# Attention values with 32-column stationary tiles, softmax sums from a block of ones, masked keys on VectorE

## What is computed

```python
q = _to_heads(plin(xm, w_q, b_q)); k = ...; v = ...      # 16 heads of 16
qt, kt, vt = (logmap0(q), logmap0(k), logmap0(v))
scores = jnp.einsum('bhqd,bhkd->bhqk', qt, kt) / math.sqrt(HD)
attn = jax.nn.softmax(scores, axis=-1)
out_h = expmap0(jnp.einsum('bhqk,bhkd->bhqd', attn, vt))
attn_out = plin(_from_heads(out_h), w_o, b_o)
x = mobius_add(residual, expmap0(g_msa * logmap0(attn_out)))
```

## Time and profile before

| | us |
|---|---|
| median of 3 runs | 1204.57 (1204.15 to 1205.57) |
| profiled execution | 1204.05 |
| its span, first to last instruction | 1202.2 |

### The profile page before, as it was taken

The page is one execution under the profiler, slowest core; times in us unless marked ns, Lnnn a source line. Parts: engine busy times, 40 slices in busy tenths (PEclk is TensorE's granted clock), DMA queues, the critical chain, the costliest instruction groups (busy, mean ns, idle before and its releaser), DMA issues.

```text
span 1202.2 us, 20974 instructions
## 1 busy us (share of the span) xinstructions
PE 1058.6 (88%) x6258; PEld 750.1 (62%) x6280; DVE 986.0 (82%) x2359; ACT 872.1 (73%) x2318; POOL 619.0 (51%) x1055
## 2 busy tenths in 40 slices
PE   7999978886995699999999999999988589898876
PEld 7888853332452377777777777777775255555544
DVE  5888769996778757888888888888867799999984
ACT  3554458886993258888888888888766888888872
POOL 2344315452777334555555555555223376767764
PEclk9999989997898689999999999999968789999998
DMA  7111110352997334444444444432443466666733
GB/s 234 54 54 53 58 62 3 146 207 86 310 383 224 106 88 106 106 106 106 105 106 106 106 106 107 106 106 54 88 106 93 83 140 141 159 158 168 173 98 123
DMA packets 113666, 147.98 MB, mean 123 GB/s; under 512 B 9232, under 2 KB 99472, under 8 KB 112784
## 3 DMA queue, kind: packets, MB, share of 16 engines
q1 hardware_dynamic: 113008, 146.64, 44.3%
q10 hardware_dynamic: 544, 0.00, 0.0%
HBM read 111.22 MB, written 27.00 MB: 115 GB/s over the span
## 4 chain that ended last, share of the span: by engine, by line
PE 39%; DVE 12%; ACT 8%; issue 6%; POOL 2%; DMA 0%; POOLq 0%; SPq 0%; DVEq 0%; ACTq 0%
PE t_bk L2029 8%; PE t_fB L2043 7%; PE t_fA L2043 7%; PE t_fB L2106 4%; PE t_bk L1386 4%; PE t_bk L2016 3%; PE t_bk L2085 2%; PE t_fB L1407 2%; DVE t_o L2377 2%; DVE t_y L2357 1%; DVE t_hsum L2361 1%; ACT t_vbd L1451 1%; ACT t_ysq L2159 1%; DVE t_qt L1619 1%; PE t_fB L2077 1%
## 5 line engine op out<-in xcount | busy, mean ns | idle before, releaser
L1386 PE MATMUL t_bk<-k_w12g,t_ut 128*128 128x512 f32 x256 | 125.7, 615 | 2.6 <-ACT t_ut L1507 1.2
L412 POOL TENSOR_SCALAR s_hleak<-k_hs,k_leak 128x128 f32<-128x128 f32 x126 | 46.9, 372 | 95.7 <-ACT k_hs L367 95.7
L2043 PE MATMUL t_fA<-k_wqkv,t_ut 128*128 128x512 f32 (+1 forms) x256 | 92.1, 504 | 1.2 <-ACT t_ut L2142 1.2
L2043 PE MATMUL t_fB<-k_wqkv,t_ut 128*128 128x512 f32 (+1 forms) x256 | 90.9, 498 | 0.0
L1958 POOL TENSOR_TENSOR t_qk<-t_y,t_fac 128x512 f32<-128x512 f32 x64 | 67.6, 1087 | 42.2 <-DVE t_fac L2435 42.2
L1386 PEld LDWEIGHTS t_bk<-k_w12g,t_ut 128*128 128x128 f32 x256 | 50.6, 198 | 53.7 <-issue 49.1
L285 PE MATMUL s_gsum<-k_hs,k_w0t 128*128 128x128 f32 x504 | 77.7, 297 | 7.0 <-ACT k_hs L367 1.1
L2377 DVE TENSOR_TENSOR t_o<-t_bk,t_rden 64x128 f32<-64x128 f32 x256 | 73.9, 289 | 8.3
L2016 PE MATMUL t_bk<-t_qbd,t_kpar 64*128 64x128 f32 x1024 | 77.1, 292 | 2.9 <-DMA t_qbd<-t_qt 1.7
L285 PEld LDWEIGHTS s_gsum<-k_hs,k_w0t 128*128 128x128 f32 x504 | 65.6, 190 | 20.8 <-ACT k_hs L367 20.3
L745 ACT ACTIVATE a_silu<-a_pg,k_wxscale 128x512 f32<-128x512 f32 x96 | 65.0, 695 | 17.6 <-PE a_pu L710 17.5
(11 more groups left out here) (383 smaller groups left out, 3141.7 us busy)
## 6 DMA issues: line engine op xcount, KB each, us to landing
t_scb<-g_rows SPq DMA_DIRECT2D x64, 256.0 KB, 4.8
t_shb<-g_rows SPq DMA_DIRECT2D x64, 256.0 KB, 5.7
hidden_rows<-k_own SPq DMA_DIRECT2D x6, 1536.0 KB, 6.0
s_xrow<-in_x_dram SPq DMA_DIRECT2D x16, 512.0 KB, 3.5
b_xin<-in_x_dram SPq DMA_DIRECT2D x16, 512.0 KB, 5.0
x_rows<-b_xout SPq DMA_DIRECT2D x16, 512.0 KB, 6.8
t_xf<-x_rows SPq DMA_DIRECT2D x16, 512.0 KB, 4.0
t_qbd<-t_qt SPq DMA_DIRECT2D x64, 128.0 KB, 2.4
```

What stands on the lines that cost most here:

```text
L1386: last = nc.tensor.matmul(z.fW[:, j, :], z.ut[:, c, j * P:(j + 1) * P], k["w12g"][:, c, :], start=False, stop=(c == C - 1))
L2043: last = nc.tensor.matmul(dst[:, w0:w1], ut[:, c, j * P:(j + 1) * P], k["wqkv"][:, c, w0:w1], start=(c == 0), stop=(c == C - 1))
```

## The change

Values are computed with the two sides exchanged. For one pair of batches (`values(n)`, four per turn) each pair of heads is a stationary tile of 32 columns of `t_vbd`, and its 64 columns of weights move; four such tiles write to four blocks of 32 partitions of one bank. Sixteen of these matmuls are followed by four that have a 128x32 block of ones (`headsum`) as stationary side and 256 moving columns: they give the softmax sum of each head, repeated over the 16 partitions of its values. The column of ones in `t_vbd` goes (VW 33 to 32). The outputs come out transposed, so `turn_o` and ACT's `turned_outputs` go, and the out-products wait for the scaled outputs directly. ACT inverts the sums (`inverse_sums(n)`: Ln, then Exp of minus that, 128x256 each, into the space of `t_o`), at four places in its order. DVE multiplies 128x256 values with them into `t_ot`, once for each pair. The four masked copies of keys move from ACT to DVE, between the `t_vbd` products and the read-out of the out-products. `wo` is loaded with its rows in another order.

```diff
-                def values(e):
-                    j, h = e // 2, e % 2
-                    if e == 0:
+                def values(n):
+                    if n == 0:
                         pe.wait_ge(s["vbd_ready"], i * 4)
-                    if e >= 2:
-                        pe.wait_ge(s["o_ready"], 2 * ((i - 1) * GB + e - 1))
-                    pe.wait_ge(s["exp_ready"], (i - 1) * EPAIRS + (e // 2 + 1))
-                    for p in range(0, PAIRS, 2):
-                        at = (p % 4 // 2 * 4 + e % 2 * C + p // 4) * 2 * T
-                        last = nc.tensor.matmul(bk[2 + e % 2][:, p * VW:(p + 2) * VW], pt[e // 2 % 2][:, at:at + 2 * T],
-                                                vbd[:, j, h, p:p + 2, :].rearrange("p c w -> p (c w)"), start=True, stop=True)
+                    if n >= 2:
+                        pe.wait_ge(s["o_ready"], (i - 1) * EPAIRS + n - 1)
+                    pe.wait_ge(s["exp_ready"], (i - 1) * EPAIRS + n + 1)
+                    for h in range(2):
+                        for c in range(C):
+                            for q in range(4):
+                                x = h * C + c
+                                nc.tensor.matmul(bk[2 + n % 2][VW * q:VW * (q + 1), x * T:(x + 1) * T], vbd[:, n, h, 4 * c + q, :],
+                                                 pt_pairs[n % 2][:, q // 2, x, q % 2, :], start=True, stop=True)
+                    for q in range(4):
+                        last = nc.tensor.matmul(bk[2 + n % 2][VW * q:VW * (q + 1), VALS:2 * VALS], headsum[:, :],
+                                                pt_pairs[n % 2][:, q // 2, :, q % 2, :], start=True, stop=True)
                     last.then_inc(s["pv_ready"], 1)
...
                 if mid:
                     values(0)
-                    values(1)
...
                     for n in range(2, EPAIRS):
                         scores(n)
-                        values(2 * n - 2)
-                        values(2 * n - 1)
...
                 if mid:
-                    values(GB - 2)
-                    values(GB - 1)
-                def turn_o(half):
-                    pe.wait_ge(s["o_ready"], 2 * ((i - 1) * GB + 4 * (half + 1)))
-                    for e in range(4 * half, 4 * half + 4):
-                        last = nc.tensor.transpose(fB[:, e * P:(e + 1) * P], o[:, e, :], k["ident"][:, :])
-                    last.then_inc(s["otp_ready"], 1)
-
+                    values(EPAIRS - 1)
...
                 if mid:
-                    turn_o(1)
+                    out_products(0)
                 if front:
+                    if mid:
+                        pe.wait_ge(s["o_ready"], i * EPAIRS)
                     turn_qk(1)
...
+                    out_products(1)
```

On ACT and DVE:

```diff
+                def inverse_sums(n):
+                    act.wait_ge(s["pv_ready"], (i - 1) * EPAIRS + (n + 1))
+                    nc.scalar.activation(rden[:, n, :], bk[2 + n % 2][:, VALS:2 * VALS], ACT.Ln).then_inc(s["dln_ready"], 1)
+                    act.wait_ge(s["dln_ready"], (i - 1) * EPAIRS + (n + 1))
+                    nc.scalar.activation(rden[:, n, :], rden[:, n, :], ACT.Exp, scale=-1.0).then_inc(s["rden_ready"], 1)
...
                 if front:
                     square_y(1)
+                if mid:
+                    inverse_sums(0)
                 if tail and i <= NG:
                     tanh_parts()
...
                     exponentials(2)
+                    inverse_sums(1)
...
                     exponentials(3)
+                    inverse_sums(2)
...
                 if mid:
-                    turned_outputs(0)
+                    inverse_sums(EPAIRS - 1)
...
-                if mid:
-                    turned_outputs(1)
-                if front:
-                    for c_ in range(C):
-                        act.wait_ge(s["qkt_ready"], i * (2 * C) + (C + c_ + 1))
-                        for par in range(2):
-                            nc.scalar.activation(kpar[:, c_, :, par, :], by_batch(bk[C + c_][:, :]), ACT.Copy,
-                                                 scale=k["mask"][:, par:par + 1]).then_inc(s["kpar_ready"], 1)
...
+                def outputs(n):
+                    dve.wait_ge(s["rden_ready"], (i - 1) * EPAIRS + (n + 1))
+                    nc.vector.tensor_tensor(ot[:, :, 2 * n:2 * n + 2, :].rearrange("p c e t -> p e c t"),
+                                            bk[2 + n % 2][:, 0:VALS].rearrange("p (e c t) -> p e c t", c=C, t=T),
+                                            rden[:, n, :].rearrange("p (e c t) -> p e c t", c=C, t=T), ALU.mult).then_inc(s["o_ready"], 1)
+
+                def keys(c):
+                    dve.wait_ge(s["qkt_ready"], i * (2 * C) + (C + c + 1))
+                    for par in range(2):
+                        nc.vector.tensor_scalar(kpar[:, c, :, par, :], by_batch(bk[C + c][:, :]), k["mask"][:, par:par + 1], None, ALU.mult).then_inc(s["kpar_ready"], 1)
...
+                if front:
+                    for c in range(C):
+                        keys(c)
                 if mid:
 
                     for c in range(C):
```

More of the change, by code:

```diff
@@ L240, in _ @@
                 r = slice(q * 2 * HD, (q + 1) * 2 * HD)
-                sp.dma_start(k["wo"][r, :, :], dr["L1_cond_w_o"].rearrange("(q c r) n -> q r c n", q=PAIRS // 2, c=C)[q]).then_inc(loaded["keep"], 16)
+                sp.dma_start(k["wo"][r, :, :], dr["L1_cond_w_o"].rearrange("(c q r) n -> q r c n", q=PAIRS // 2, c=C)[q]).then_inc(loaded["keep"], 16)
             with nc.allow_non_contiguous_dma(reason="vectors of a few hundred values, once"):
@@ L1695, in attention_mlp @@
         ptile = m.sb("pt", [P, 4 * D])
-        rden = m.sb("rden", [P, 4, PAIRS // 2, 2])
+        headsum = m.sb("headsum", [P, VW])
         o = m.sb("o", [P, GB, P])
@@ L1743, in attention_mlp @@
         pt = (ptile[:, :], flat_qt)
+        pt_pairs = [x.rearrange("p (r x b t) -> p r x b t", r=2, x=2 * C, b=2) for x in pt]
+        VALS = 2 * C * T
         flat_qbd = qbd[:, :, :, :].rearrange("p c q r -> p (c q r)")
@@ L1939, in _ @@
                 start.do(pool.memset(t, 0.0))
-            start.do(pool.memset(vbd[0:T, :, :, :, 2 * HD].rearrange("p j h (q c) -> p (j h) q c", c=2)[:, :, :, 0], 1.0))
-            pool.memset(vbd[T:2 * T, :, :, :, 2 * HD].rearrange("p j h (q c) -> p (j h) q c", c=2)[:, :, :, 1], 1.0).then_inc(s["zero_ready"], 1)
+            start.do(pool.memset(headsum[:, :], 0.0))
+            start.do(pool.memset(headsum[0:T, 0:HD], 1.0))
+            pool.memset(headsum[T:2 * T, HD:2 * HD], 1.0).then_inc(s["zero_ready"], 1)
             pool.wait_ge(s["zero_ready"], 1)
@@ L2064, in turn @@
                         scores(n)
-                        values(2 * n - 2)
-                        values(2 * n - 1)
+                        values(n - 1)
                 if i == NG:
@@ L2087, in turn_qk, with out_products @@
                                 last.then_inc(s["qkt_ready"], 1)
-                if mid:
-                    if front:
+                def out_products(half):
+                    if front and half == 0:
                         pe.wait_ge(s["y_ready"], (i + 1) * GT)
-                    turn_o(0)
+                    for j in (2 * half, 2 * half + 1):
+                        pe.wait_ge(s["o_ready"], (i - 1) * EPAIRS + j + 1)
+                        for c in range(C):
+                            last = nc.tensor.matmul(fB[:, j * D:(j + 1) * D], ot[:, c, 2 * j:2 * j + 2, :].rearrange("p e t -> p (e t)"), k["wo"][:, c, :],
+                                                    start=(c == 0), stop=(c == C - 1))
+                    last.then_inc(s["yop_ready"], 1)
                 if front:
@@ L2097, in turn @@
                 if mid:
-                    turn_o(1)
+                    out_products(0)
                 if front:
+                    if mid:
+                        pe.wait_ge(s["o_ready"], i * EPAIRS)
                     turn_qk(1)
                 if mid:
-                    for j in range(GT):
-                        if j % 2 == 0:
-                            pe.wait_ge(s["ot_ready"], (i - 1) * C + j // 2 + 1)
-                        for c in range(C):
-                            last = nc.tensor.matmul(fB[:, j * D:(j + 1) * D], ot[:, c, 2 * j:2 * j + 2, :].rearrange("p e t -> p (e t)"), k["wo"][:, c, :],
-                                                    start=(c == 0), stop=(c == C - 1))
-                        if j % 2:
-                            last.then_inc(s["yop_ready"], 1)
+                    out_products(1)
             pe.wait_ge(s["const_ready"], 1)
@@ L2248, in turn @@
                     once(second.turned_u, 0)
[L2249 to L2252 removed]
                 if mid:
[L2255 removed]
+                    inverse_sums(EPAIRS - 1)
+                if i == NG - 1:
+                    scales_a.scalar_root(act)
                 if front:
@@ L2411, in turn @@
                 if mid:
-                    outputs(0, 2)
```

(8 more changed lines are left out.)

35 lines of the change are left out of this document (7 added, 28 removed).

## The result

The changed kernel takes 1235.24 us (median of 4 runs, 1232.89 to 1235.79) against 1204.36 for the kernel before, run beside it: a ratio of 1.0244, 95% interval 1.022 to 1.0269. The profiled execution took 1235.35 us, its span is 1233.6, 31.4 more than before.

A forecast was written before the change was run, and what follows sets the result against it. The prediction took the ACT, DVE and POOL hand-off to bound the changed kernel: 13 intervals at +4.95 us (+64.4), +1.4 for turn 1, +4.2 and -2 at the end, about +68, so 1272 us; range 1240 to 1318.

The forecast's parts named there:

- DVE's wait for the inverse ahead of its last output: Sign expected in the changed kernel's timeline: DVE waits for ACT's `t_o` before its last output; no size given.
- PE's wait for DVE: Sign expected in the changed kernel's timeline: PE waits for DVE before its second product; no size given.
- the sum: Loop steps between fourth squares gave 34.95 us for 30.00; 13 intervals at +4.95, plus both ends, together +68 us.
- `t_vbd` 4.46 us: Value-tile products on DVE, between last output and keys: taken to last 4.46 us, from 11.7 to 16.15 in the loop.
- V = 2.0: Value matmuls on PE: 2.0 us for one pair of batches, no gain; bounds 1.1 and 4.5.
- Factor two from the row blocks: Overlap of value matmuls in column blocks on PE, taken from the scores' row blocks: 3.4 us becomes 1.7.
- rival 1: Column blocks of the value matmuls on PE don't overlap: a pair takes 3.4 to 4.5 us, 1316 or 1380 us; chance 0.15.
- Inverse pairs 0.90: Ln and Exp over 256 columns on ACT, four times per turn: 0.90 us each, bounds 0.8 and 1.1.
- Keys 0.65 each: Four masked key copies on DVE ahead of `t_yo`: 0.65 us each, 2.6 us together.
- Outputs 0.42: Four output products of 128x256 on DVE: 0.42 us each, between 0.289 and 0.715.
- Rival 2: PE's clock falls to 1.2 GHz, last scores and values take 3.1 us more: 1292 or 1312 us; chance 0.08.
- Rival 4: Smaller loss: POOL's chain overlaps, copies are quicker, a pair's values take 1.1 us; period 33, about 1244 us; chance 0.08.

The follow-up runs named there:

- e1: The changed kernel with the four masked key copies back on ACT, behind the queries' copies: 1206.25 us, ratio 1.001.
- e7: The changed kernel with two of the four masked key copies on ACT and two on DVE: 1214.31 us, ratio 1.0069.
- e11: The changed kernel with only the first pair of inverse sums moved behind the tanh operations, keys still on DVE: 1213.48 us, ratio 1.005.
- e5: The changed kernel with keys back on ACT and the first pair of inverse sums behind the tanh operations: 1196.5 us, ratio 0.9909.
- e6: The changed kernel with three unused 512-column matmuls on PE in the gap ahead of the last scores: 1222.65 us, ratio 1.0135.
- e8: The kernel before, with POOL's residual add waiting until DVE has built the value tiles: 1206.04 us beside 1208.41, ratio 0.9983.
- e9: The changed kernel with the value matmuls ordered block by block instead of going round the four column blocks: 1232.43 us, ratio 1.0213.
- e4: The changed kernel with sums inverted by reciprocals on DVE and keys back on ACT: 1213.93 us, ratio 1.0078.
- e14: As e5, with the last pair of inverse sums moved ahead of the copies of `t_ut`: 1194.62 us beside 1208.41, ratio 0.9888.

## Why the forecast was right in sign and wrong in size

**The bound and the mechanism: right.** The changed kernel is bound by the hand-off between ACT, DVE and POOL. The keys ahead of `t_yo` (e1, e7) and the first inverse pair ahead of POOL's chain (e11, e5) were named in the prediction, and each moved the time when it was moved. The path closes through `inverse` and the fourth square, as written. Of the signs that were named, DVE's wait for the inverse ahead of its last output came (4.45 us); PE's wait for DVE came 0.54 us long ahead of the first scores, for the keys, not ahead of the second product.

**Where the size failed.** At a clock of 1.00, which the sum assumed, the loop is 31.52 us (turn 2, e6) where I had 34.95: 3.43 too much. The largest terms in it are `t_vbd` (1.24) and the values on PE (0.8); four inverse pairs add 0.6, and the rest is in small pieces of 0.1 to 0.3. The fall of the clock, which the sum left out, then gave about 1.3 back.

**`t_vbd` 4.46 us: the first step that failed.** It took 3.20 to the keys. I took a merged row of four for the work of four, where one of them had stood for 1.6 us behind POOL's add (e8). The row's neighbour on POOL, at 660.68, was in the same timeline. The Trainium skill has the rule ("SBUF — State Buffer", section "SBUF: two separate sides"): DVE operations with two SBUF inputs and GpSimd operations that read SBUF take a shared port pair for a whole instruction, and the other blocks. The trace agrees: 2.28 us began inside POOL's add and 0.69 without it.

**Values, V = 2.0: the second.** A pair takes 1.08 us, the lower end. Factor two from the row blocks was too low a bound for four column blocks; the 0.3 for drain and changes of shape is seen in no run by itself. In the loop V = 2.0 held the third inverse pair back to 1.7 us behind the start of the last exponential; at a clock of 1.00 it starts 0.9 us behind it (473.48 and 474.39 in turn 2), without a wait for PE. That values can stand in the loop is shown by e9: with 1.82 for a pair the wait is there, and the turn is 0.7 us longer. The rule that made rival 1, in the Trainium skill, "TensorE: Matmul & The Clock Gate", Part 3 (a load overlaps matmuls only in another row group), does not hold here: 40 loads and 40 matmuls, all on four row groups, take 1.08 us. Rival 1 is dead.

**Inverse pairs 0.90: measured 0.74 to the next operation** (659.36 to 660.10 for `tanh_parts`). Four of them in the loop: -0.6. The way from second to fourth square was 7.11 in place of 7.5, in part for this.

**Keys 0.65 each: 2.64 for four to `t_yo`, as taken.** Outputs 0.42: 0.42.

**Rival 2, the clock: partly right, in the place that was named.** The clock falls in each of the turns 3 to 14, not in half of them. It does not always fall at the same place: the last scores take 2.07 or 2.08 us in five of these turns, 1.81 to 1.85 in three, and 1.16 in four, where it falls behind them. Turns 3 to 13 are 32.1 to 33.3 us long, against 31.52, so the price is at most 1.76 and on average 1.3 us, where rival 2 had 3.1. I had held it apart as an alternative; it came on top and hid how much too dear the other terms were.

**Rival 4 was nearest, and in part by luck.** Its period of 33 and its 1244 us lie close to 32.7 and 1235, and its V of 1.1 is what came. But at a clock of 1.00 the kernel is at 31.5, and the step from there to 32.7 is the clock, which that rival did not name.

**The sum.** Twelve intervals at +2.69 where +4.95 was forecast: 27 of the missing 37 us. The two first intervals gave -1.66 and +1.51 where +1.4 and +4.95 stood: 6.5. In turn 1 there is no add on POOL and no tail. Behind turn 15 it was -0.5, where +4.2 - 2 stood: 2.7.

**Left open.** What decides in which turn the clock falls: with a gap of 2.7 us ahead of the last scores e7 has turns with and without a fall, e11 has none with 2.1, and e4 has eight with no gap over 0.91. And why e1, e5 and e14 take 6 to 8 us more behind turn 15.

## What to carry to other kernels

Before an operation's duration is carried into a new schedule, take its single instructions apart, and look what the other engines do during the longest one; a merged row can hold a wait that the new order removes or brings back. In a pipeline of engines with fixed queues the place of a small operation counts, not its sum: 0.74 us moved out of POOL's chain gave 22 us, and 2.6 us of copies moved from ACT to DVE cost 29. When an engine leaves the bound, what it saves returns as gaps. In this kernel PE's clock then fell in 12 turns, and work that filled a gap won 12.6 us. Before turns are compared or a term is priced, sort them by the granted clock: the turns at 1.00 gave each experiment's own effect (31.52, 30.21, 29.72), the means mixed it with the clock's.

## What the runs showed of the hardware

- A DVE product of two SBUF operands (0.69 us) that starts inside a two-operand add on POOL ends 0.55 us after the add ends: 2.28 us. Apart in time, all 60 take at most 0.691 (e8).
- The reverse is seen too, though no run tested it, and POOL's times are rough. Most of POOL's small operations take 0.20 us, but the one that meets DVE's product of two SBUF operands takes over 1 us, in the chain that ACT's `inverse` waits for (kernel before; in the changed one it is 1.14 us at 662.46):

```profile
649.12 1.29 POOL L1206 TENSOR_TENSOR t_s_den<-k_sq,t_s_th 128x4 f32<-128x4 f32 x1
649.14 1.22 DVE L2329 TENSOR_TENSOR t_u<-t_u,t_scb 128x1024 f32<-128x1024 f32 x1
```

- Four column blocks of 32 run side by side if neighbours in the queue are in different blocks: 32 records of 64 columns start within 0.44 us.
- Reciprocal of 128x256 f32 from PSUM on DVE: 1.75 us. Ln and then Exp on ACT: 0.79.
- With a gap of 2.8 us on PE ahead of the last scores the granted clock fell in turns 3 to 14, and the same 16 records took up to 2.08 us in place of 1.16. With a gap of 2.1 us (e11) they took 1.16 in every turn. The length of the gap alone does not decide it: see what is left open.
